# A graph layer's last stage: attention projection as three f32r products, and a row quantiser in another element order

## The reference

```python
xn  = layernorm(x)
gnn = segment_softmax_attention(rmsnorm(xn) @ W_down, src, dst) @ W_up     # 4 heads, self loops added
q, k, v = xn @ Wq + bq, xn @ Wk + bk, xn @ Wv + bv                        # 16 heads of 64
kv  = sum over rows of phi(k)^T v, per head                               # phi(t) = elu(t) + 1
mix = (phi(q) @ kv) @ Wo + bo
x1  = x + gnn + mix
def fake_quant(t, s):                                                     # per block of 16 elements
    sc8 = e4m3(clip(max|t| / 6 * s, 0, 448)); dq = sc8 / s
    return round_to_fp4(clip(t / dq, -6, 6)) * dq
h   = layernorm(x1)
hid = silu(fake_quant(h) @ fake_quant(gate)^T) * (fake_quant(h) @ fake_quant(up)^T)
out = x1 + fake_quant(hid) @ fake_quant(down)^T
```

## Time and profile before

| | |
|---|---|
| runs (us) | 1056.94, 1059.74, 1411.92; median 1059.74 |
| profiled execution | 1058.53 us, span 1056.8 us |
| granted PE clock, mean | 0.967 |
| busy in the span | PE 91%, DVE 79%, ACT 61%, POOL 47% |

### The profile page before, as it was taken

How to read it: one execution, slowest core, us unless ns; L and a number is a source line. 1 busy time by engine, 2 the same in 40 slices (tenths; PEclk the granted TensorE clock), 3 DMA queues, 4 the chain that set the end, 5 groups by cost and what they waited for, 6 DMA issues and landing times. The chain is left out here.

```text
span 1056.8 us, 17499 instructions
## 1 busy us (share of the span) xinstructions
PE 959.5 (91%) x5429; PEld 794.3 (75%) x5429; DVE 837.9 (79%) x1395; ACT 648.7 (61%) x1435; POOL 496.7 (47%) x582
## 2 busy tenths in 40 slices
PE   2698879999999999999997779999999879999986
PEld 2676779999999999999997357888898334454443
DVE  5875567888888888888888868998995768887776
ACT  3274446665765766666664568999898335554442
POOL 0211777777777777777771524444444200110000
PEclk9699889999999999999998899999999989999998
DMA  9304588989889898998872689989985364674314
GB/s 246 56 7 110 169 243 259 292 265 280 257 254 294 266 287 284 288 280 282 277 244 91 247 198 332 293 278 310 290 270 192 79 135 122 149 160 112 81 19 79
DMA packets 109977, 221.40 MB, mean 209 GB/s; under 512 B 25883, under 2 KB 58228, under 8 KB 109857
## 3 DMA queue, kind: packets, MB, share of 16 engines
q1 hardware_dynamic: 89053, 159.98, 47.2%
q0 software_dynamic: 20576, 60.08, 23.8%
q10 hardware_dynamic: 260, 0.20, 0.1%
HBM read 156.56 MB, written 62.95 MB: 208 GB/s over the span
## 5 line engine op out<-in xcount | busy, mean ns | idle before, releaser
L1024 POOL DMA_INDIRECT score_gath<-xl_rows,misc x324 | 347.4, 1072 | 101.6 <-issue 92.1
L1064 PE MATMUL score_ps_m<-x_hi,score_w_hi 128*128 128x416 f32 (+1 forms) x576 | 209.4, 363 | 2.1 <-DVE score_w_lo L1217 1.9
L1065 PE MATMUL score_ps_m<-x_lo,score_w_hi 128*128 128x416 f32 (+1 forms) x576 | 204.1, 354 | 0.0
L1066 PE MATMUL score_ps_m<-x_hi,score_w_lo 128*128 128x416 f32 (+1 forms) x576 | 204.1, 354 | 0.0
L1784 ACT ACTIVATE agg_gath<-agg_gath,prob 128x64 f32<-128x64 f32 x648 | 159.2, 353 | 6.7 <-DMA agg_gath<-edge_rows 6.4
L1196 DVE TENSOR_TENSOR score_zb<-score_gath,score_ps_x 128x1024 f32<-128x1024 f32 x81 | 98.8, 1219 | 67.6 <-PE score_ps_x L1047 57.9
L1733 PE MATMUL ps_all<-agg_gath,agg_hot 128*125 128x128 f32 x648 | 128.0, 280 | 9.8 <-DVE agg_hot L1839 6.4
L1735 PE MATMUL ps_all<-agg_gath,agg_hot 128*125 128x136 f32 x648 | 128.9, 281 | 0.0
L1733 PEld LDWEIGHTS ps_all<-agg_gath,agg_hot 128*125 128x125 f32 x648 | 100.5, 189 | 25.8 <-issue 25.2
L2081 PE MATMUL ps_all<-mix_w,phi_c 128*125 128x512 f32 x240 | 108.4, 602 | 5.8 <-DVEq L2355 5.2
L1064 PEld LDWEIGHTS score_ps_m<-x_hi,score_w_hi 128*128 128x128 f32 x576 | 109.7, 190 | 4.2 <-issue 2.6
(11 more groups left out here) (341 smaller groups left out, 1666.3 us busy)
## 6 DMA issues: line engine op xcount, KB each, us to landing
edge_rows<-score_gath SPq DMA_DIRECT2D x81, 528.0 KB, 3.8
agg_gath<-edge_rows SPq DMA_DIRECT2D x81, 528.0 KB, 5.6
local_bc<-local_rows SPq DMA_DIRECT2D x40, 224.0 KB
score_gath<-xl_rows,misc POOLq DMA_INDIRECT x324, 4.5
...
```

Of the source, the lines that this page charges most:

```text
L1024: nc.gpsimd.indirect_dma_start(out=gath[:, g % GS, q, :], out_offset=None, in_=xl_rows, in_offset=bass.IndirectOffsetOnAxis(ap=src_idx[:, ...
L1064: pe.matmul(acc, w_hi[:, i % 2, kk, :], x_hi[:, kk, cols], start=(kk == 0), stop=False)
L1065: pe.matmul(acc, w_hi[:, i % 2, kk, :], x_lo[:, kk, cols], start=False, stop=False)
L1066: mm = pe.matmul(acc, w_lo[:, i % 2, kk, :], x_hi[:, kk, cols], start=False, stop=(kk == KC - 1))
```

## The change

It has five parts.

1. In the last stage each f32 product of `mix_part` becomes three f32r products: high by high, high by remainder, remainder by high (L2157 to L2159). The first chunk's projection goes wholly into the aggregation (`EARLY` changes from 4, 3, 3, 3, 3, 2, 2 to 8, 2, 2, 2, 2, 2, 2: again 40 early products, in f32). The wait for the turned graph rows moves behind the first half's products.
2. Phi is split per chunk: ACT copies the high part (`high_phi`, L2318), DVE subtracts for the remainder (`low_phi`, L2395).
3. `mix_w` is split tile by tile. Six tiles are split on POOL in the aggregation, in groups 22, 30, 38, 46, 54 and 62 (`split_early`: a copy, L1745, and a subtraction, L83); the high parts of three of them go to DRAM and are read back by SP at the start of the last stage, since SBUF has no room earlier. The last two tiles are copied by ACT (`split_high`, L2321) and subtracted by POOL at the start of the last stage.
4. The row quantiser works in another element order: element s of block n stands at place 32 s + n of a run of 512, so that a scale row is read with step 1. ACT's normalise and DVE's hidden row write in that order (f32, a step of 128 bytes), the block maxima read at that step, and the products of `PairQuantiser` write the weights in the same order.
5. In the row quantiser the clip moves behind the pull, onto bf16, and the product is bf16 by bf16.

```diff
-EARLY = [4, 3, 3, 3, 3, 2, 2] + [0] * (NC - 7)
+EARLY = [KC] + [2] * 6 + [0] * (NC - 7)
+SPLIT = [2, 3, 4, 5, 6, 7, 0, 1]
+SPLIT_EARLY = 6
+SPLIT_KEPT = 3
+def split_low(nc, k, n, high):
+    kk = SPLIT[n]
+    nc.gpsimd.tensor_tensor(k.mix_lo[:, kk, :], k.mix_w[:, kk, :], high[:, :].bitcast(F32), ALU.subtract).then_inc(k.s_mix_lo, 1)
...
+LANES = 32
+def by_lane(ap):
+    return ap.rearrange("p (b s n) -> p b n s", s=16, n=LANES)
+def natural(ap):
+    return ap.rearrange("p (b n s) -> p b n s", s=16, n=LANES)
...
     def product(self, out, j):                                   # PairQuantiser, weights
-        return self.v.tensor_tensor(self.blocks(out), self.blocks(self.work), self.wide(0, j), ALU.mult)
+        return self.v.tensor_tensor(by_lane(out), natural(self.work), scale.unsqueeze(3).to_broadcast([P, 2, LANES, 16]), ALU.mult)
...
+                def split_early(n):
+                    kk = SPLIT[n]
+                    pool.wait_ge(s_piece, 2)
+                    if n > SPLIT_KEPT:
+                        pool.wait_ge(k.s_mix_kept, 16 * (n - SPLIT_KEPT))
+                    high = k.mix_hi[kk] if n < SPLIT_KEPT else mix_stage
+                    nc.gpsimd.tensor_copy(high[:, :], k.mix_w[:, kk, :]).then_inc(k.s_mix_hi, 1)
+                    pool.wait_ge(k.s_mix_hi, n + 1)
+                    split_low(nc, k, n, high)
+                    if n >= SPLIT_KEPT:
+                        nc.gpsimd.dma_start(k.mix_rows[n - SPLIT_KEPT, :, :], mix_stage[:, :].bitcast(F32)).then_inc(k.s_mix_kept, 16)
                 for g in range(NG):
                     extras(g)
+                    for n in range(SPLIT_EARLY):
+                        if g == 22 + 8 * n:
+                            split_early(n)
...
-        q.do(v.tensor_reduce(amax, x.rearrange("p (n s) -> p n s", s=16), AX.X, ALU.max, apply_absolute_value=True))
+        q.do(v.tensor_reduce(amax.rearrange("p (b n) -> p b n", n=LANES), by_lane(x), AX.X, ALU.max, apply_absolute_value=True))
...
-        q.do(v.tensor_scalar(a, a, 6.0, -6.0, ALU.min, ALU.max))          # clip, behind the scaling
...
-        q.do(v.scalar_tensor_tensor(out=a, in0=b, scalar=COARSE, in1=a, op0=ALU.max, op1=ALU.subtract))
+        q.do(v.scalar_tensor_tensor(out=b, in0=b, scalar=COARSE, in1=a, op0=ALU.max, op1=ALU.subtract))
+        q.do(v.tensor_scalar(b, b, 6.0, -6.0, ALU.min, ALU.max))
...
                 def mix_part(c, half):
                     for kk in range(EARLY[c], KC):
-                        pe.matmul(ps_y[0:C, half, :], phi_c[:, c % 2, kk, :], mix_w[:, kk, half * 512:half * 512 + 512],
-                                  start=(kk == EARLY[c]), stop=False)
+                        high, low = phi_hi[:, c % 2, kk, :], phi_lo[:, c % 2, kk, :]
+                        pe.matmul(ps_y[0:C, half, :], high, k.mix_hi[kk][:, cols], start=(kk == EARLY[c]), stop=False)
+                        pe.matmul(ps_y[0:C, half, :], high, k.mix_lo[:, kk, cols], start=False, stop=False)
+                        pe.matmul(ps_y[0:C, half, :], low, k.mix_hi[kk][:, cols], start=False, stop=False)
...
-                    act.activation(h, x1[:, c % 3, :], ACT.Identity, bias=shift, scale=rstd).then_inc(s_h, 1)
+                    act.activation(by_lane(h), natural(x1[:, c % 3, :]), ACT.Identity, bias=shift, scale=rstd).then_inc(s_h, 1)
...
                 copy_gnn(6)
                 copy_gnn(7)
+                for n in range(6, KC):
+                    split_high(n)
+                high_phi(2)
                 size_x(0)
...
                     clip_x(c)
                     round_h(c - 2)
+                    if c + 2 < NC:
+                        low_phi(c + 2)
                     round_x(c)
```

More of the change, by code:

```diff
@@ L199, in allocate_late @@
     k.agg_gath = ctx.enter_context(nc.sbuf_tensor("agg_gath", [P, AGG_SLOTS, GP, XW], F32))
+    gath_bytes = 4 * AGG_SLOTS * GP * XW
+    k.gath_at = nc.sbuf_base - gath_bytes
+    assert 4 * D * (KC - SPLIT_KEPT + 1) <= gath_bytes
+    k.s_mix_lo = ctx.enter_context(nc.semaphore("s_mix_lo"))
+    k.s_mix_hi = ctx.enter_context(nc.semaphore("s_mix_hi"))
+    k.s_mix_kept = ctx.enter_context(nc.semaphore("s_mix_kept"))
+    k.s_mix_back = ctx.enter_context(nc.semaphore("s_mix_back"))
+    k.mix_rows = nc.dram_tensor("mix_rows", (SPLIT_EARLY - SPLIT_KEPT, P, D), F32, kind="Internal").ap()
+    homes = [k.parts_at, k.parts_at + 4 * D, k.kv_at] + [k.gath_at + 4 * D * n for n in range(KC - SPLIT_KEPT)]
+    k.mix_lo = nc.alloc_sbuf_tensor_at("mix_lo", [P, KC, D], F32R, offset=k.mix_at)
+    k.mix_hi = {kk: nc.alloc_sbuf_tensor_at(f"mix_hi{kk}", [P, D], F32R, offset=at) for kk, at in zip(SPLIT, homes)}
     k.prob = ctx.enter_context(nc.sbuf_tensor("prob", [P, PB * P, HEADS], F32))
@@ L1876, in __init__, with wide, scale_row @@
         self.v, self.q, self.amax, self.small, self.work, self.coarse = v, steps, amax, small, work, coarse
+    def wide(self, row, width):
+        return row.rearrange("p (b n) -> p b n", n=LANES).unsqueeze(2).to_broadcast([C, width // 512, 16, LANES])
+    def scale_row(self, width):
+        return self.small[0:C, 2, :].bitcast(BF16)[:, 0:width // 16]
     def scales(self, x, width):
@@ L1996, in finish @@
         s_tail = sem("s_tail")
+        s_phi_hi = sem("s_phi_hi")
+        s_phi_lo = sem("s_phi_lo")
         s_pself = sem("s_pself")
@@ L2018, in _ @@
             def _(sp):
+                for n in range(SPLIT_KEPT, SPLIT_EARLY):
+                    sp.wait_ge(k.s_mix_kept, 16 * (SPLIT_EARLY - SPLIT_KEPT))
+                    sp.dma_start(k.mix_hi[SPLIT[n]][:, :].bitcast(F32), k.mix_rows[n - SPLIT_KEPT, :, :]).then_inc(k.s_mix_back, 16)
                 sp.wait_ge(k.s_part, 16 * 2 * (NP_CHUNKS - 2))
@@ L2063, in _ @@
                         complete_x(c + 2)
+                    if c == 0:
+                        for n in range(6, KC):
+                            pool.wait_ge(k.s_mix_hi, n + 1)
+                            split_low(nc, k, n, k.mix_hi[SPLIT[n]])
                     if 0 <= c - 3 < NC - 1:
@@ L2086, in gnn_part @@
                         m = pe.matmul(ps_y[0:C, half, :], gnn_t[:, kk, C * c:C * c + C], w_up[:, kk, half * 512:half * 512 + 512],
-                                      start=False, stop=(kk == 1))
+                                      start=(kk == 0 and EARLY[c] == KC), stop=(kk == 1))
                     if half:
@@ L2154, in stay_warm @@
                         pe.matmul(ps_y[0:C, 0, :], ident_b[:, 0:C], k.gate_q[:, 1, :, 0, :], start=True, stop=True)
-                pe.wait_ge(s_phi[0], 16)
-                for half in range(2):
-                    mix_part(0, half)
                 turn_gnn(0)
@@ L2242, in _, with high_phi, split_high @@
                 act.activation(tail[:, :], ps_all[0:C, 5, 0:2 * HALF + UPPER], ACT.Copy).then_inc(s_tail, 1)
+                def high_phi(c):
+                    act.wait_ge(s_phi[c % 2], 16 * (c // 2 + 1))
+                    act.activation(phi_hi[:, c % 2, EARLY[c]:, :], phi_c[:, c % 2, EARLY[c]:, :], ACT.Copy).then_inc(s_phi_hi, 1)
+                def split_high(n):
+                    act.activation(k.mix_hi[SPLIT[n]][:, :], mix_w[:, SPLIT[n], :], ACT.Copy).then_inc(k.s_mix_hi, 1)
+                high_phi(1)
                 act.wait_ge(s_eps, 1)
@@ L2303, in _, with low_phi @@
                 v.sem_inc(s_den, 1)
+                def low_phi(c):
+                    part = phi_c[:, c % 2, EARLY[c]:, :]
+                    v.wait_ge(s_phi_hi, c)
+                    v.tensor_tensor(phi_lo[:, c % 2, EARLY[c]:, :], part, phi_hi[:, c % 2, EARLY[c]:, :].bitcast(F32),
+                                    ALU.subtract).then_inc(s_phi_lo, 1)
+                low_phi(1)
                 v.wait_ge(s_pself, 1)
@@ L2371, in clip_x @@
                     quant_x.scales(h, D)
-                    quant_x.clipped(h, D)
+                    quant_x.scaled(h, D)
                     v.sem_inc(s_clip_x, 1)
@@ L2385, in hidden @@
                     v.wait_ge(s_g, b + 1)
-                    own.do(v.scalar_tensor_tensor(out=hid[:, :], in0=ps_g[0:C, 1, :], scalar=fs[0:C, 6:7], in1=e[:, :],
-                                                  op0=ALU.mult, op1=ALU.mult))
+                    own.do(v.scalar_tensor_tensor(out=by_lane(hid[:, :]), in0=natural(ps_g[0:C, 1, :]), scalar=fs[0:C, 6:7],
+                                                  in1=natural(e[:, :]), op0=ALU.mult, op1=ALU.mult))
                     v.sem_inc(s_hid, 1)
                 def clip_h(b):
-                    quant_h.clipped(hid[:, :], FF)
+                    quant_h.scaled(hid[:, :], FF)
                     v.sem_inc(s_clip_h, 1)
```

54 lines of the change are left out of this document (34 added, 20 removed).

## The result

The changed kernel takes 1126.29 us (median of four runs) against 1058.82; the ratio is 1.0647, 95% interval 1.0620 to 1.0674. The ratio leaves out one slow run of the kernel before, of 1411.92 us. Forecast were 1066 us and a range up to 1090. The profiled execution took 1125.62 us, span 1123.9, 67.1 more than the span before.

The account below looks back on a forecast made before the run. The prediction took PE, ACT and DVE as full in the aggregation, DVE's round as the floor before chunk 6, PE behind it. Terms -7.6 - 1.3 - 1.6 + 6 + 0.5 + 7 + 5 = +8 on 1058.5 gave 1066 us, range 1046 to 1090.

Parts of the forecast that it names:

- S: Strided accesses of the by-lane quantiser, in aggregation and last stage: reads free, writes at half, +5 us (ends 0 and +22).
- The upper end, +22: Strided-access cost if every strided f32 or bf16 stream, reads included, slows by a factor 1.76: +22 us together.
- strided reads and writes are slow: Rival: strided accesses cost +22 instead of +5, DVE's round passing PE's behind chunk 6; 1083 us, chance 0.27.
- A: Six weight splits on POOL in the aggregation: 23.4 us holding DVE, 9 arriving, fewer late pieces giving 3 back; +6 us.
- C: Head of the last stage: ACT's weight and phi copies (2.9 us), then POOL's two subtractions holding DVE; +7 us.
- F: Projection behind chunk 6: three f32r products replace each f32 one, PE rounds 20.55 instead of 23.07; -7.6 us.
- E: Rounds from chunk 2 to 6, set by DVE: phi remainder added, clip and product cheaper; -1.3 us before strided accesses.
- B: Head of the last stage: chunk 0's products leave, a phi remainder joins DVE's chain; +0.5 us (-1 to +3).
- G: Tail behind chunk 9: cheaper x product, clip and two hidden rows, no phi remainder; -1.6 us.

Follow-up runs that it names:

- experiment 1: The changed kernel with only the twelve weight products of the quantiser writing in natural order again: 1089.09 us, ratio 1.0293 to the kernel before.
- experiment 3: The changed kernel with natural element order everywhere (weights, normalise, hidden row, maxima), all else as changed: 1073.94 us, ratio 1.0175 to the kernel before.
- experiment 4: The kernel before with weight products, normalises and maxima in varied element orders per call; f32 maximum 1.22 us at 8-byte steps, 1.88 to 2.00 from 16.
- 6: The changed kernel with natural order everywhere and the last two weight splits moved, their subtractions from POOL to DVE: 1071.40 us, ratio 1.0108 to the kernel before.
- experiment 5: The kernel before with the new early-piece distribution: 1067.07 us; plus unread POOL copies and subtractions: 1078.88; with POOL copies only instead: 1083.02.

## Why the prediction was wrong

**S, the strided accesses: the step that failed.** "I take reads at 0, since a strided read is the row that there is, and writes at half": the row was a read of PSUM, and it said nothing of SBUF. The term was +5 and measured about 49: 35.3 in the aggregation (experiment 1), and some 14 behind it (experiment 1 against 3, from the start of the last stage to the end: 257.3 and 243.3 us, already net of the halved product). ACT's normalise, which S names among the strided writes, had no price in it at all and took 1.03 us more in each round, with DVE waiting for it. The upper end, +22, was wrong too. The factor 1.76 fits f32 (reads 1.65, ACT's writes 1.83), but it was applied to the bf16 write of the weights as well, which slowed by 3.86: 3.47 us more on each of twelve instructions, where 0.92 was the bound. The rival "strided reads and writes are slow" had the right mechanism and place, DVE's round passing PE's behind chunk 6, and a time of 1083 to 1090 because of that bound. The rule that the prediction quoted from the Trainium skill (page "Vector Engine (DVE) Microarchitecture Reference", section 5.2) was right in kind (but for the step of 8 bytes, experiment 4) and was given too little weight: it speaks of SBUF, the row did not. The term came out above even the +40 that the prediction worked out from the page's largest figure.

**A, the six splits.** The mechanism was right and the size was not: +6 taken, +12 as the end; 14.8, 11.2 and 17.4 us are left in experiments 1, 3 and 6, and POOL work of that kind alone costs 11.8 by the medians (experiment 5). Two terms were mis-sized. The first is the idle time that was to take up all but 9 of 23.4 us of hold: DVE was busy 16.5, 13.0 and 17.3 us longer in those three, less than 23.4, but next to none of it was taken up. The 10 us in the second window took up next to nothing; they lie at the end of the aggregation, most of them behind DVE's last group, as the prediction itself had noted, and in all these runs DVE is busy 43 to 45 of the last 55 us. The second is the 3 us that fewer late pieces were to give back: experiment 5 shows 0.5 (815.74 against 816.28), in an execution below its median. The durations were good: 2.66 for 2.6, 1.03 for 1.3:

```profile
L83 POOL TENSOR_TENSOR mix_lo<-mix_w,mix_hi 128x1024 fp32r<-128x1024 f32 x5 | 12.9, 2663 | 0.2
...
L1745 POOL CAST mix_hi<-mix_w 128x1024 fp32r<-128x1024 f32 x3 | 3.1, 1034 | 0.0
```

**C, the head of the last stage**: +7 forecast, +7.5 measured, and shown by moving the splits away. The sum was better than its parts: the hold was 5.3 us (6.20 for an instruction of 0.94) and not "some 4 of 5.2 us", so ACT's copies cost less than the 2.9 taken. That the two errors cancel is luck.

**F, the projection**: 0.23 us a product and PE rounds of 20.5 were right, seen where PE sets the pace (experiments 3 and 6). The changed kernel does not get there, since DVE's round was not "below 20 us" but 21.4: -4.9 in place of -7.6.

**E**: the parts came as worked out, the product halved (0.69), the clip on bf16 0.43, the remainder of phi 0.94; the strides and ACT's normalise (1.03 more, on which DVE waits) turned a round of 18.7 into 21.4. One reading was loose: the products before were 10, 10, 12 and 12 for chunks 3 to 6, not 12 in most; the sum goes by the products after the change, so nothing hangs on it. In natural order the product would not have halved (experiment 3).

**B**: +2.0 for +0.5, within its ends. **G**: the tail gained 1.0 in natural order and lost 1.9 by lane.
